# Feed-forward stage: three of the four down-weight pieces of odd units in attention buffers, and the down products of step 14 placed behind the last gate and up products

## The reference

```
x = x + layernorm(attention(layernorm(x)))        # linear attention, 16 heads on 4 key heads, rope, elu + 1
h = silu(x1n @ w_gate) * (x1n @ w_up)             # x1n = layernorm(x), inner width 2048
h_sparse = of every 4 neighbours of h, keep the 2 of largest magnitude
x = x + layernorm(h_sparse @ w_down)
```

## Time and profile before

| what | value |
|---|---|
| median of 3 runs | 1372.93 us (1369.69 to 1373.05) |
| the profiled execution | 1372.72 us, of which the span is 1370.9 |
| TensorE busy | 1255.4 us, 92% |
| VectorE busy | 956.3 us, 70% |
| GpSimd busy | 668.5 us, 49% |
| ScalarE busy | 567.2 us, 41% |
| first down product starts | 820.18 us |
| first down product of the last unit starts | 1314.21 us |

### The profile page before, as it was taken

How to read it: one execution, slowest core, us unless ns; L and a number is a source line. 1 busy time by engine, 2 the same in 40 slices (tenths; PEclk the granted TensorE clock), 3 DMA queues, 4 the chain that set the end, 5 groups by cost and what they waited for, 6 DMA issues and landing times.

```text
span 1370.9 us, 15339 instructions
## 1 busy us (share of the span) xinstructions
PE 1255.4 (92%) x5496; PEld 1011.8 (74%) x5496; DVE 956.3 (70%) x1434; ACT 567.2 (41%) x994; POOL 668.5 (49%) x516
## 2 busy tenths in 40 slices
PE   5679999999999899999997899999999989999994
PEld 4457777778787687777785678788787868787873
DVE  6368787787788787878777666666556755555566
ACT  3255555555554645555645323233322232323220
POOL 4146565555577655556546544242325452424234
PEclk9799999999999999999999999999999999999998
DMA  4232132121232322212212221120203220202102
GB/s 165 51 88 62 39 85 55 46 62 47 77 99 83 91 66 86 53 48 71 53 31 93 77 85 55 38 85 31 77 24 115 77 93 16 77 16 77 32 32 77
DMA packets 50059, 90.26 MB, mean 66 GB/s; under 512 B 6464, under 2 KB 6720, under 8 KB 49984
## 3 DMA queue, kind: packets, MB, share of 16 engines
q1 hardware_dynamic: 49984, 89.29, 22.5%
HBM read 64.09 MB, written 8.39 MB: 53 GB/s over the span
## 4 chain that ended last, share of the span: by engine, by line
PE 56%; DVE 23%; ACT 7%; issue 6%; POOL 3%; DMA 3%; SPq 1%; POOLq 0%; DVEq 0%
PE bank_q L371 5%; PE bank_q L373 5%; PE bank_q L372 5%; PE bank_o L371 4%; PE bank_o L373 3%; PE bank_o L372 3%; PE bank_t L371 2%; PE bank_t L372 2%; PE bank_t L373 2%; PE bank_y L373 2%; PE bank_y L372 2%; PE bank_y L371 2%; PE bank_s L371 2%; PE bank_s L373 2%; PE bank_s L372 2%
## 5 line engine op out<-in xcount | busy, mean ns | idle before, releaser
L923 POOL TENSOR_TENSOR big_lo<-scratch,big_hi 128x1024 fp32r<-128x1024 f32 (+1 forms) x64 | 150.5, 2361 | 243.7 <-ACT big_hi L675 228.2
L923 POOL TENSOR_TENSOR w_lo<-stage,w_hi 128x512 fp32r<-128x512 f32 x96 | 138.9, 1455 | 117.6 <-ACT w_hi L589 117.6
L371 PE MATMUL bank_q<-x_hi,w_hi 128*128 128x512 f32 x448 | 180.8, 404 | 16.0 <-DVE scratch L745 9.1
L373 PE MATMUL bank_q<-x_lo,w_hi 128*128 128x512 f32 x448 | 178.3, 398 | 0.0
L372 PE MATMUL bank_q<-x_hi,w_lo 128*128 128x512 f32 x448 | 178.0, 397 | 0.0
L923 POOL TENSOR_TENSOR s_lo<-scratch,s_hi 128x512 fp32r<-128x512 f32 x64 | 92.7, 1448 | 140.9 <-ACT s_hi L625 140.9
L666 ACT ACTIVATE scratch<-scratch 128x512 f32<-128x512 f32 x64 | 40.5, 632 | 269.5 <-DVE scratch L872 269.5
L923 POOL TENSOR_TENSOR a_lo<-scratch,a_hi 128x512 fp32r<-128x512 f32 x64 | 83.0, 1297 | 97.9 <-ACT a_hi L644 97.9
L371 PE MATMUL bank_y<-wout_hi,a_hi 128*128 128x512 f32 x256 | 102.9, 402 | 13.7 <-POOL wout_lo L923 9.7
L371 PEld LDWEIGHTS bank_q<-x_hi,w_hi 128*128 128x128 f32 x448 | 86.5, 193 | 35.7 <-POOL w_lo L923 7.1
L373 PE MATMUL bank_y<-wout_lo,a_hi 128*128 128x512 f32 x256 | 101.3, 396 | 0.0
(11 more groups left out here) (191 smaller groups left out, 3410.8 us busy)
## 6 DMA issues: line engine op xcount, KB each, us to landing
scratch<-scratch SPq DMA_DIRECT2D x128, 128.0 KB, 2.3
x_rows<-x SPq DMA_DIRECT2D x56, 256.0 KB, 2.9
stage<-wq SPq DMA_DIRECT2D x32, 256.0 KB, 2.7
stage<-wo SPq DMA_DIRECT2D x32, 256.0 KB, 2.6
stage<-wg SPq DMA_DIRECT2D x32, 256.0 KB, 2.6
stage<-wu SPq DMA_DIRECT2D x32, 256.0 KB, 2.7
stage<-wd SPq DMA_DIRECT2D x32, 256.0 KB, 2.6
x<-x_rows SPq DMA_DIRECT2D x16, 256.0 KB, 2.5
```

The costliest lines, as they stand in the source:

```text
L371: pe.matmul(ps, whi, xhi, start=first, stop=False, skip_group_check=True)
L373: return pe.matmul(ps, whi, xlo, start=False, stop=last, skip_group_check=True)
L923: return pool.tensor_tensor(dst, full, hi.bitcast(F32), ALU.subtract)
```

## The change

It has three parts.

1. Pieces 0, 1 and 2 of odd units go to the attention buffers k_t, a and v (`Dh`, `Dl`); those of even units stay in `wout`. So they wait only for the down products of unit u - 2. They are split in ticks 8u + 1, 8u + 2 and 8u + 3. Piece 3 stays in one buffer for all units, in tick 8u + 5 (4 for unit 0).
2. Pieces 0 to 2 are subtracted on GpSimd, piece 3 on VectorE.
3. Down products 56 to 63 (steps 14 and 15) are done in ticks 64 to 71 instead of 61 to 68, so ticks 61 to 63 have gate and up products alone. The sums of the second batch's row blocks move with them, from ticks 61 to 68 to ticks 64 to 71, and `TICKS` is three longer.

```diff
-TICKS = [("a", s) for s in range(-7, 65)] + [("f", 0), ("a", 65)] + [("f", n) for n in range(1, 71)]
+TICKS = [("a", s) for s in range(-7, 65)] + [("f", 0), ("a", 65)] + [("f", n) for n in range(1, 74)]
...
+def down_at(n):
+    y = n - 5 if n <= 60 else n - 8 if n >= 64 else -1
+    return y if 0 <= y < SLOTS else None
...
-    return tick_f(32 * b + 29 + t)
+    return tick_f(64 + t if b else 29 + t)
...
     for u in range(UNITS):
-        plan += [(("d", u, i), tick_f(8 * u + 5 if u else 2)) for i in range(4)]
+        plan += [(("d", u, i), tick_f(8 * u + 1 + i)) for i in range(3)]
+        plan += [(("d", u, 3), tick_f(8 * u + 5 if u else 4))]
...
 def by_dve(piece):
-    return piece[0] in "od" and piece[2] < 2
+    return piece[0] == "o" and piece[2] < 2 or piece[0] == "d" and piece[2] == 3
...
+        Dh = [KTh[:, :, :].rearrange("p c d -> p (c d)"), Ah[:, :, :].rearrange("p c d -> p (c d)"),
+              Vh[:, :, :].rearrange("p c d -> p (c d)")[:, 0:W]]
+        Dl = [KTl[:, :, :].rearrange("p c d -> p (c d)"), Al[:, :, :].rearrange("p c d -> p (c d)"),
+              Vl[:, :, :].rearrange("p c d -> p (c d)")]
...
-            kind, _, i = piece
+            kind, u, i = piece
+            if kind == "d" and u % 2 and i < 3:
+                return Dh[i], Dl[i]
             if kind in "od":
                 return Oh[:, i, :], Ol[:, i, :]
...
-                y = n - 5
-                if 0 <= y < SLOTS:
+                y = down_at(n)
+                if y is not None:
...
+                        wh, wl = dest(("d", y // 8, i))
                         ins = three(psYF[y % 2][:, :], big_h[:, d % 2, i, ts * P:(ts + 1) * P],
-                                    big_l[:, d % 2, i, ts * P:(ts + 1) * P], Oh[:, i, :], Ol[:, i, :],
-                                    i == 0, i == 3)
+                                    big_l[:, d % 2, i, ts * P:(ts + 1) * P], wh, wl, i == 0, i == 3)
...
                 elif kind == "d":
-                    g.wait_ge(pe_d, 8 * u)
+                    g.wait_ge(pe_d, 8 * u - (0 if i == 3 else 8))
                     g.wait_ge(pe_y, SLOTS)
```

## The result

The changed kernel takes 1339.88 us (median of 4 runs, 1337.37 to 1340.82) where the kernel before takes 1371.87 us (4 runs, 1369.69 to 1373.05): a ratio of 0.9766, 95% interval 0.975 to 0.9781. It is faster by 2.3%. The forecast was 1340.8 us.

A forecast was written before the change was run, and what follows sets the result against it. TensorE, busy 92% of the span, was taken as the bound. Boundaries (26.1 us) and tail (6.0) take 32.1 off 1370.9, giving 1338.8, or 1340.8 us as measured median; range 1337 to 1346, over the cases 1335 to 1351.

The forecast's parts named there:

- The boundaries: Late down products once per eight-step unit, waiting for down-weight low parts; 26.1 us gained up to step 61's up product.
- The moved pieces: Pieces 0 to 2, split in ticks 8u+1 to 8u+3; extra ScalarE and GpSimd work hidden, costed at 0.
- the sum: Whole forecast: 26.1 us at boundaries plus 6.0 in the tail, 32.1 off the 1370.9 us span.
- The remainders: Boundary losses expected to stay after the change, mainly at units 1 and 4: 3.0 us.
- boundaries 1 to 6: Unit starts before the last unit's; gaps and slower matmuls after them were said to cost 29.1 us.
- The margin of 0.4 us: Piece 3 ready 1.62 us after the up product, needed at 2.05, in units 2, 3, 5 and 6.
- The tail: From step 61's up product to the end: 6.0 us gained, VectorE and GpSimd row loop at 3.10 us per block.
- The moved down products alone: Down products put behind the last up product in the tail; worth 1.4 us of its 6.0.
- boundary 7: Start of the last unit, at y = 56: a 2.17 us gap plus slow matmuls, 4.6 us gained.
- The wait that moves to piece 3: Rival at unit boundaries: queues hold piece 3 longer than 2.05 us in every unit; about 1350 us, chance 0.16.
- The tail that yields nothing: Rival: row loop slower than 3.10 us or hid starves in steps 61 to 63; 1348 us, chance 0.08.
- Slower, by low parts on GpSimd: Rival in ticks 8u+1 to 8u+3: VectorE held off or ScalarE waiting, hid late; 1375 us or more, chance 0.03.

The follow-up runs named there:

- e4: Changed kernel's buffers and relaxed wait, but all four pieces split in tick 8u+5 on the old engines, down products in old ticks: 1371.4 us, ratio 1.0.
- e8: Changed kernel with two more, unused subtractions on VectorE ahead of piece 3's low part in each unit: 1347.3 us, ratio 0.983.
- e3: Changed kernel with low parts on the engines of before, pieces 0 and 1 on VectorE, 2 and 3 on GpSimd: 1340.2 us, ratio 0.9784.
- e2: Kernel before with only the down products and row sums moved, pieces as they were: 1367.2 us, ratio 0.9976.
- e9: Changed kernel plus four PSUM banks and pipelined row loop, with piece 3's low part ahead of row add and statistics on VectorE: 1334.4 us, ratio 0.9728.
- e1: Changed kernel with down products and row sums back in their old ticks, so only the pieces are moved: 1339.6 us, ratio 0.9775.
- e5: Changed kernel with four PSUM banks in turn for down products 56 to 63: 1339.3 us, ratio 0.9765.
- e6: Changed kernel with row loop pipelined from tick 64, add and statistics of a block before normalising the previous one: 1340.0 us, ratio 0.9777.

## Why the prediction was right

**The boundaries.** Forecast: 491.9 us become 465.8, by 26.1. Measured: 467.0, by 24.9. The 1.2 us between them are what three larger errors leave, and that they nearly cancel is luck:

- The moved pieces cost 1.8 us where the sum had nothing. I priced them by who waits for their splits and did not ask what it costs TensorE that they lie in other buffers (e4).
- The remainders I had kept were 3.0 us: 0.3 at unit 1, 1.6 of wait and 0.8 of slow clock at unit 4, 0.3 elsewhere. The trace has 1.3, all at unit 4 (1.10 of idle time, a start that is 1.27 late), with a granted clock of 1.00 behind it. That is 1.7 too much.
- Of the 29.1 us that I gave to boundaries 1 to 6, 1.1 are no boundary's. They are left in the changed kernel when the transposes, the small gaps, unit 4 and the slower steps of odd units are taken off, and the kernel before has them too: in units 0, 2, 4 and 6, away from the boundaries, each down product takes the same time in both, to 2 ns.

The margin of 0.4 us that I worked out from VectorE's queue for units 2, 3, 5 and 6 is 0.37 to 0.45 in e8 for units 3, 5 and 6. For unit 2 it is 0.04: VectorE starts there 1.18 us after the up product (955.57 - 954.39) and not 0.88. That no gap shows at unit 2 was close to chance.

**That time counts, and not place.** I argued that nothing ahead of piece 3 in VectorE's queue moves and that pieces 0 to 2 must be early. e4 shows the second half: the buffers alone give a ratio of 1.0. It also corrects a reason that the prediction gave: at the boundary ScalarE was held by its own queue and no longer by the buffers that y = 55 reads. e3 shows that the choice of engine is free. Of the moved splits I said that they lie under idle time; there is no new gap in ticks 8u + 1 to 8u + 4.

**The tail.** Forecast from the up product of step 61 to the end: 52.9 us; measured 53.1. Its parts, counted from that product: first row add at 24.15, measured 1309.72 - 1285.54 = 24.18; gap 8.4 us, measured 8.24; restart 5.33 us for y = 58, measured 1315.74 - 1310.46 = 5.28; 3.10 per row block, measured 3.11; 7.09 behind the last add, measured 7.11. Reading the order in VectorE's queue (ranking, big_lo, then the row add that frees a bank) was what kept me from the 8 us that four down products behind the last up product seem to promise.

**What was off.** The moved down products alone I put at 1.4 us: 0.7 in the traces, nothing that the times can show. The 4.6 us of boundary 7 do not come in full when the moved products alone remove it: e2 gets 3.3 us in all by the times and 4.0 in the traces, since the hidden product of step 60 stands behind the splits (1.54 us of wait). GpSimd is busy 3.5 us more and not 10. And the span fell by 32.3 us where the sum said 32.1, but 1.6 of that is the earlier start of the first down product. From there on it is 550.7 - 520.0 = 30.7 us, so the forecast of the total was a little too high and met by chance.

**The rivals.** The wait that moves to piece 3 did so in unit 4 only; e8 shows what more lateness would have cost: 8.1 us in the traces for 0.9 to 1.3 us at each boundary. The tail that yields nothing: nearly so for the moved products, but by a loop at 3.11 us that did not slow down. Slower, by low parts on GpSimd that hold VectorE off: no wait of TensorE shows it in the ticks in which they now are, though e9 shows that the mechanism exists where the two meet on the path.

## What to carry to other kernels

Where a product waits for a weight piece, look at what stands ahead of its split in each engine's queue before giving it another buffer: the buffer alone gained nothing (e4), the earlier tick that it allows gave 2.2% (e1). Compare the pace of the matmuls with the new buffer and with the old one, too: here it cost 1.8 us that no wait shows. Before counting work that is put behind a wait as cover, follow what frees the banks and who sets the pace after it: a gap of TensorE that was cut from 10.0 to 8.2 or to 2.7 us was worth 0.7 us or less as long as a loop of two other engines at 3.1 us per block came behind. Two limits of nearly the same height hide each other: e5 and e6 gave 0.1 and 0.7 us alone and 4.8 together.

## What was not expected of the hardware

TensorE's pace depends on the buffer that a down piece lies in: 216 matmuls take 49.66 us where the down pieces lie in `kt`, `a` and `v`, and 49.13 where all lie in `wout`, at a granted clock of 1.00 and without an idle stretch in either. The cause stays open. With most pauses gone the granted clock of the stage rose from 0.98 to 1.00: TensorE ran at the upper level from 818 to 1290, 472 us in which it was busy for all but 2.0. And one subtraction of 128 x 512 on VectorE takes 0.66 us alone and 1.78 beside a GpSimd add, so that moving it forward in its queue by three instructions (e9) gained 1.5 us of start and lost 1.1 of duration.
